# A transformer layer on eight cores: residual rows on ScalarE's DMA queue, another order ahead of the heads, and two more tiles turned by DMA

## The reference

```python
lat = rmsnorm(x @ wkv_a_w.T, norm_w)
kv = lat @ wkv_b_w.T
q = (x @ wq_w.T + wq_b).reshape(B, S, H, DH)
...
attn = softmax(where(tril, (q @ k.T) / sqrt(DH), -inf))
x = x + (attn @ v) @ out_w.T + out_b
...
gate = silu(qmm(x, gate_w, gate_scale)); up = qmm(x, up_w, up_scale)
x = x + qmm(gate * up, down_w, down_scale)
```

## Time and profile before

| | us |
|---|---|
| median of three runs | 1604.93 |
| lowest and highest of them | 1598.73 and 1613.68 |
| the profiled execution | 1596.11 |
| its span on the slowest core (core 1) | 1594.4 |
| spans of cores 0 to 7 | 1591.8, 1594.4, 1592.5, 1590.4, 1592.4, 1593.8, 1591.9, 1589.6 |
| busy on core 1: PE, DVE, ACT, POOL | 1555.1, 440.4, 363.7, 82.0 |
| the stages on core 1 begin at | heads 133.4, output rows 490.3, gate and up 596.6, down 1259.6 |

### The profile page before, as it was taken

How to read it: one execution, slowest core, us unless ns; L and a number is a source line. 1 busy time by engine, 2 the same in 40 slices (tenths; PEclk the granted TensorE clock), 3 DMA queues, 4 the chain that set the end, 5 groups by cost and what they waited for, 6 DMA issues and landing times.

```text
span 1594.4 us, 22671 instructions; the slowest of 8 cores (1589.6 to 1594.4 us)
## 1 busy us (share of the span) xinstructions
PE 1555.1 (98%) x8714; PEld 758.8 (48%) x8714; DVE 440.4 (28%) x998; ACT 363.7 (23%) x480; POOL 82.0 (5%) x174
## 2 busy tenths in 40 slices
PE   3999999999999999999999999999999999999999
PEld 2644555555555444444444444444444444444444
DVE  5735444444456661111011110111011111111111
ACT  3864565656662001101110011101110000000000
POOL 1210100000100000000000000000000000000000
PEclk9999999999999999999999999999999999999999
DMA  9953445222456995352754565372532383929210
GB/s 277 288 96 77 71 83 87 44 34 41 78 100 185 142 199 119 31 49 27 63 44 44 50 52 50 35 63 27 48 32 27 27 115 53 124 52 119 69 53 27
DMA packets 75752, 127.60 MB, mean 80 GB/s; under 512 B 46144, under 2 KB 48768, under 8 KB 70912
## 3 DMA queue, kind: packets, MB, share of 16 engines
q0 software_dynamic: 17856, 58.73, 36.6%
q1 hardware_dynamic: 57792, 67.42, 15.0%
HBM read 233.08 MB, written 16.78 MB: 157 GB/s over the span
## 4 chain that ended last, share of the span: by engine, by line
PE 91%; DMA 5%; DVE 2%; issue 1%; SPq 1%; ACT 0%; POOL 0%; DVEq 0%; ACTq 0%; POOLq 0%
PE PS L1342 21%; PE PS L1317 21%; PE PS L1323 21%; PE PS L1113 7%; PE PS L1192 4%; PE PS L1168 4%; PE PS L1122 3%; PE PS L1132 3%; PE PS L1077 3%; PE PS L1299 2%; DMA X2T<-XHb 2%; DMA WST<-wkva 1%; DMA res_scr<-RES 1%; PE PS L1141 1%; DMA X<-xq 1%
## 5 line engine op out<-in xcount | busy, mean ns | idle before, releaser
L1317 PE MATMUL PS<-X2T,W 128*128 128x512 bf16 x1536 | 347.2, 379 | 0.0
L1323 PE MATMUL PS<-X2T,W 128*128 128x512 bf16 x1536 | 347.2, 379 | 0.0
L1317 PEld LDWEIGHTS PS<-X2T,W 128*128 128x128 fp8e4 x1536 | 150.3, 98 | 181.2
L1323 PEld LDWEIGHTS PS<-X2T,W 128*128 128x128 fp8e4 x1536 | 150.3, 98 | 181.3
L880 DVE SCALAR_TENSOR_TENSOR FUSE<-PS,CF,SIL 128x512 bf16<-128x512 f32 x96 | 72.1, 751 | 587.4 <-PE PS L1323 587.4
L1032 ACT ACTIVATE SIL<-PS,CF 128x512 bf16<-128x512 f32 x96 | 66.0, 687 | 589.6 <-PE PS L1317 589.6
L957 ACT ACTIVATE P<-PS,NEGB 128x1024 bf16<-128x1024 f32 x192 | 169.9, 900 | 115.1 <-PE PS L1168 104.9
L1342 PE MATMUL PS<-WDb,FUSE 128*128 128x512 fp8e4 (+2 forms) x816 | 166.2, 366 | 0.0
L1342 PE MATMUL PS<-WDa,FUSE 128*128 128x512 fp8e4 x768 | 166.1, 379 | 0.0
L1342 PEld LDWEIGHTS PS<-WDb,FUSE 128*128 128x128 bf16 x816 | 77.9, 98 | 88.3
L1342 PEld LDWEIGHTS PS<-WDa,FUSE 128*128 128x128 bf16 x768 | 75.2, 98 | 90.6
(11 more groups left out here) (123 smaller groups left out, 946.5 us busy)
## 6 DMA issues: line engine op xcount, KB each, us to landing
W<-gu POOLq DMA_DIRECT2D x48, 512.0 KB, 9.0
WQ<-wq POOLq DMA_DIRECT2D x16, 512.0 KB, 6.7
X<-xo SPq DMA_DIRECT2D x8, 1024.0 KB, 9.1
WO<-wo POOLq DMA_DIRECT2D x16, 512.0 KB, 8.8
RES<-xq SPq DMA_DIRECT2D x8, 1024.0 KB, 7.5
res_scr<-RES SPq DMA_DIRECT2D x8, 1024.0 KB, 6.5
RB<-res_scr SPq DMA_DIRECT2D x32, 256.0 KB, 5.3
out<-OB SPq DMA_DIRECT2D x31, 256.0 KB, 2.4
```

Of the source, the lines that this page charges most:

```text
L1317: mm = e.matmul(bank(ffn_bank(f)), W8[io % 4][:, c * 128:(c + 1) * 128], X2T[:, c * 1024 + qb * 512:c * 1024 + qb * 512 + 512], start=(c = ...
L1323: mm = e.matmul(bank(ffn_bank(f) + 1), W8[io % 4][:, 2048 + c * 128:2048 + (c + 1) * 128], X2T[:, c * 1024 + qb * 512:c * 1024 + qb * 512 ...
```

## The change

It has these parts:

- **Tiles 9 and 10** are no longer transposed on PE and evicted by ACT. They are turned by DMA, as two half turns each, between the loads of tiles 12, 13 and 14 in SP's queue (`TURNED`, `turn_late`). PE waits for the landing of a turned tile where it waited for ACT (`turned`), and so does whoever writes over its XH buffer (`slot_free`).
- **Who normalises**: ACT has tiles 7 to 10; DVE has the others, 12 to 15 among them. Before, ACT had 8 to 10 and 12 to 15.
- **SP's loads**: X3 goes ahead of the first two WST, WST3 ahead of X7.
- **POOL**: WQ's load moves behind `rstd(4)`, WK's behind `rstd(8)`, and WV's behind `rstd(9)`.
- **PE's list** ahead of the heads is in another order: `rope_sum` is first; 20 and 6 matmuls of 512 columns whose results nothing reads (`warm`) are put ahead of tile 2 and behind tile 5; `lat(0, 0)`, `lat(2, 1)`, `lat(3, 0)` and `lat(3, 1)` are split, and `lat(1, ...)` no longer is; parts of `lat(3, ...)` come earlier. DVE's and ACT's lists follow it.
- **Output rows**: the spills and the RES loads of tiles 4 to 7 are issued by ACT between its roots. The load of tile t + 3 is issued after spill t, when spill t - 1 has landed.

The diff, cut in its lines of context, and without the declarations of semaphores:

```diff
@@ -82,7 +82,8 @@
-NORM_ON_ACT = (8, 9, 10, 12, 13, 14, 15)
+NORM_ON_ACT = (7, 8, 9, 10)
+TURNED = (9, 10, 12, 13, 14, 15)
...
@@ -136,7 +137,7 @@
 KIND_COUNT = {
-    "T": lambda n, half: 2 * n + half + 1,
+    "T": lambda n, half: 2 * sum(1 for k in range(n) if k not in TURNED) + half + 1,
     "Q": lambda h, qb: 2 * h + qb + 1,
...
@@ -405,6 +407,16 @@
+    def turned(n):
+
+        if n in TURNED:
+            return [(d_late[n - 8], 16)] + ([(d_late2[n - 8], 16)] if n < 12 else [])
+        return [(s_t, count(("T", n, 1)))]
+
+    def slot_free(n):
+
+        return turned(n) if n in TURNED else [(t_t, count(("T", n, 1)))]
+
     def x_count(n):
...
@@ -444,10 +456,22 @@
             src = xq_d if n < 8 else xo_d
             e.dma_start(out=X[n % 4][:, :], in_=src.ap()[(n % 8) * 128:(n % 8 + 1) * 128, :]).then_inc(d_x[n % 4], 16)
 
+        def load_constants():
+            e.dma_start(out=CF[:, :], in_=cf_d.ap()[:, :]).then_inc(d_const, 16)
+            e.dma_start(out=C2s[0:64, :], in_=c2_d.ap()[:, :]).then_inc(d_const, 16)
+            e.dma_start(out=M2s[0:64, :], in_=m2_d.ap()[:, :]).then_inc(d_const, 16)
+
         def turn_late(n):
             e.wait_ge(*normalised(n))
-            e.dma_start_transpose(out=A(XOTL, (n - 12) * 128, [[8192, 128], [512, 16], [1, 128]]),
-                                  in_=XH[n - 12][:, :]).then_inc(d_late[n - 12], 16)
+            e.wait_ge(s_cast, 4)
+            if n < 12:
+                for half in range(2):
+                    e.dma_start_transpose(out=A(XOT[half], (n - 8) * 128, [[4096, 128], [512, 8], [1, 128]]),
+                                          in_=XH[n % 4][:, half * 1024:(half + 1) * 1024]
+                                          ).then_inc((d_late if half == 0 else d_late2)[n - 8], 16)
+            else:
+                e.dma_start_transpose(out=A(XOTL, (n - 12) * 128, [[8192, 128], [512, 16], [1, 128]]),
+                                      in_=XH[n % 4][:, :]).then_inc(d_late[n - 8], 16)
 
         def load_wkva(dl):
             e.dma_start(out=WST[dl][:, :], in_=wkva_d.ap()[dl, :, :]).then_inc(d_wkva[dl], 16)
...
@@ -457,25 +481,25 @@
                         in_=xq_d.ap()[0:128, half * 1024:(half + 1) * 1024]).then_inc(d_first[half], 16)
         e.dma_start(out=CB[:, :], in_=cb_d.ap()[:, :]).then_inc(d_idb, 16)
         load_x(1)
-        e.dma_start(out=CF[:, :], in_=cf_d.ap()[:, :]).then_inc(d_const, 16)
-        e.dma_start(out=C2s[0:64, :], in_=c2_d.ap()[:, :]).then_inc(d_const, 16)
-        e.dma_start(out=M2s[0:64, :], in_=m2_d.ap()[:, :]).then_inc(d_const, 16)
+        load_constants()
         load_x(2)
+        load_x(3)
         load_wkva(0)
-        load_x(3)
         load_wkva(1)
         load_x(4)
         load_x(5)
         load_wkva(2)
         load_x(6)
+        load_wkva(3)
         load_x(7)
-        load_wkva(3)
         load_x(8)
         load_x(9)
         load_x(10)
         load_x(11)
         load_x(12)
+        turn_late(9)
         load_x(13)
+        turn_late(10)
         load_x(14)
         load_x(15)
         turn_late(12)
...
@@ -508,14 +532,9 @@
         for t in range(8):
-            e.wait_ge(v_add, 4 * (t + 1))
-            e.dma_start(out=res_d.ap()[t * 128:(t + 1) * 128, :], in_=RES[t % 4][:, :]).then_inc(d_spill[t % 4], 16)
             e.wait_ge(v_xh, 16 - len(NORM_ON_ACT) + t + 1)
                                   in_=XH2[t % 2][:, :]).then_inc(d_turn[t % 2], 16)
-            if t < 4:
-                e.wait_ge(d_spill[t % 4], 16)
-                load_res(t + 4)
         for i in range(4):
...
@@ -577,16 +596,16 @@
         rstd(2)
-        first_weights(0)
-        first_weights(1)
         rstd(3)
         rstd(4)
+        first_weights(0)
         rstd(5)
         rstd(7)
+        rstd(8)
+        first_weights(1)
+        rstd(9)
         first_weights(2)
-        rstd(8)
-        rstd(9)
         rstd(10)
...
@@ -660,7 +679,8 @@
             if n >= 4:
-                e.wait_ge(t_t, count(("T", n - 4, 1)))
+                for wait in slot_free(n - 4):
+                    e.wait_ge(*wait)
             e.tensor_scalar(XH[n % 4][:, :], X[n % 4][:, :], MV[:, 2 * n:2 * n + 1], RSTD[:, n:n + 1],
...
@@ -772,40 +792,42 @@
         stats(0)
         stats(1)
         normalise(0)
+        rope_squares()
         normalise(1)
         stats(2)
+        stats(3)
         normalise(2)
-        stats(3)
         normalise(3)
-        rope_squares()
         stats(4)
+        stats(5)
         normalise(4)
-        stats(5)
         normalise(5)
         stats(6)
         normalise(6)
+        stats(7)
         rope_weights()
-        stats(7)
-        normalise(7)
+        diagonal(0)
         stats(8)
         stats(9)
         stats(10)
-        diagonal(0)
+        evict(PLANNED[0])
         stats(11)
         latent(0)
+        stats(12)
         normalise(11)
-        evict(PLANNED[0])
-        stats(12)
         stats(13)
+        normalise(12)
         diagonal(1)
         stats(14)
+        normalise(13)
         stats(15)
+        normalise(14)
+        normalise(15)
         latent(1)
         diagonal(2)
         latent(2)
         diagonal(3)
         evict(PLANNED[11])
-        value_ones()
         latent(3)
         evict(PLANNED[13])
         evict(PLANNED[14])
...
@@ -817,8 +839,9 @@
         evict(PLANNED[21])
+        evict(PLANNED[24])
         evict(PLANNED[23])
-        evict(PLANNED[24])
+        value_ones()
         def add(t, d):
...
@@ -911,8 +934,9 @@
             e.wait_ge(g_shift, normalised(n)[1])
-            if 4 <= n and n - 4 < 12:
-                e.wait_ge(t_t, count(("T", n - 4, 1)))
+            if n >= 4:
+                for wait in slot_free(n - 4):
+                    e.wait_ge(*wait)
             e.activation(XH[n % 4][:, :], X[n % 4][:, :], AFT.Identity, bias=SHIFT[:, n:n + 1],
...
@@ -960,58 +984,53 @@
         e.wait_ge(v_eps, 1)
         e.activation(SDL[:, 0:1], EPSC[:, 0:1], AFT.Sqrt)
         transposed(0)
+        transposed(1)
         cast(0)
-        transposed(1)
-        cast(1)
         transposed(2)
         transposed(3)
+        cast(1)
         cast(2)
         transposed(4)
         e.wait_ge(d_const, 48)
         lat_out(0, 0)
+        lat_out(0, 1)
+        cast(3)
+        lat_out(0, 2)
         transposed(5)
-        cast(3)
-        transposed(6)
-        lat_out(0, 1)
-        transposed(7)
-        lat_out(0, 2)
         lat_out(0, 3)
         rms(0)
+        normalise(7)
+        transposed(6)
+        transposed(7)
         normalise(8)
         normalise(9)
         lat_out(1, 0)
+        transposed(8)
+        lat_out(1, 1)
+        lat_out(1, 2)
         normalise(10)
-        lat_out(1, 1)
-        transposed(8)
-        lat_out(1, 2)
-        transposed(9)
+        evict(PLANNED[1])
         lat_out(1, 3)
         evict(PLANNED[2])
-        evict(PLANNED[1])
-        transposed(10)
+        evict(PLANNED[3])
         rms(1)
-        evict(PLANNED[3])
         transposed(11)
-        normalise(12)
-        normalise(13)
         evict(PLANNED[4])
         lat_out(2, 0)
-        normalise(14)
+        lat_out(2, 1)
         evict(PLANNED[5])
-        normalise(15)
-        lat_out(2, 1)
-        evict(PLANNED[6])
-        evict(PLANNED[7])
-        evict(PLANNED[8])
         lat_out(2, 2)
         lat_out(2, 3)
+        evict(PLANNED[7])
+        evict(PLANNED[6])
+        lat_out(3, 0)
+        lat_out(3, 1)
+        evict(PLANNED[8])
+        lat_out(3, 2)
+        rms(2)
         evict(PLANNED[9])
+        lat_out(3, 3)
         evict(PLANNED[10])
-        lat_out(3, 0)
-        rms(2)
-        lat_out(3, 1)
-        lat_out(3, 2)
-        lat_out(3, 3)
         rms(3)
         evict(PLANNED[12])
         evict(PLANNED[17])
...
@@ -1025,6 +1044,12 @@
                     evict(job)
         for t in range(8):
             sqrt_var(16 + t)
+            e.wait_ge(v_add, 4 * (t + 1))
+            e.dma_start(out=res_d.ap()[t * 128:(t + 1) * 128, :], in_=RES[t % 4][:, :]).then_inc(d_spill[t % 4], 16)
+            if 1 <= t < 5:
+                e.wait_ge(d_spill[t - 1], 16)
+                e.dma_start(out=RES[t - 1][:, :],
+                            in_=xq_d.ap()[(t + 3) * 128:(t + 4) * 128, :]).then_inc(d_r[t - 1], 16)
         for f, (io, qb) in enumerate(FFN):
             e.wait_ge(t_g, f + 1)
             if f >= 3:
...
@@ -1036,6 +1061,10 @@
                 e.wait_ge(*evicted(before))
+
+        def warm(n):
+            for _ in range(n):
+                e.matmul(bank(3), IDB, CB[:, 0:512], start=True, stop=True)
...
@@ -1067,13 +1096,11 @@
                     e.wait_ge(s_lat, dl + 1)
                 else:
                     e.wait_ge(s_lat, 4 * tb + dl - 1)
-            if tb < 3:
-                e.wait_ge(s_t, 8 * tb + hi // 64)
-            else:
-                for i in range(hi // 128):
-                    e.wait_ge(d_late[i], 16)
+            for n in range(4 * tb, 4 * tb + hi // 128):
```

(69 more changed lines are left out.)

## The result

| | before | after |
|---|---|---|
| median (us) | 1602.55 | 1654.53 |
| ratio, with its 95% interval | | 1.031 [1.026, 1.036] |
| the profiled execution | 1596.11 | 1658.78 |
| span of the slowest core (core 1 in both) | 1594.4 | 1657.0 |
| lowest span of a core | 1589.6 | 1588.4 |

The medians here and in the table of the experiments count every execution, while the ratios leave out those in which one die ran longer at a lower granted clock (without its one such execution, the median of after is 1650.3).

A forecast was written before the change was run, and what follows sets the result against it. PE's list bounds the kernel, with almost unbroken matmuls after `scores(0)`. Gains of 2.9 us ahead of it and 2.5 in core 1's output rows leave core 5 slowest, 3.5 off the span: 1604.9 - 3.5 = 1601.4 us, whole range 1592 to 1611.

The forecast's parts named there:

- Output rows: Moving spills and later RES loads to ACT's queue removes PE's wait: 2.5 us on core 1, 0 elsewhere.
- a turn alone on SP's queue isn't held by the spill: Output rows: the reason given for taking the 2.5 us gain on core 1.
- The next square root is all that stands behind it: Output rows, ACT: the wait for a spill, one tile (13.8 us) after its issue, holds up only that root.
- Rival 2: Output rows: the spill's move is worth nothing and the 2.5 us stays; 1602.0 us, chance 0.15.
- Head of the stage: Work ahead of the heads: `scores(0)` comes 2.9 us earlier, from 0.5 + 1.8 + 1.2 - 0.6.
- The walk: PE's list on core 1 ahead of the heads, timed step by step: a lead of 0.5 us beside the 1.8.
- no wait at 80: Latent stage: PE was forecast to wait 0.6 us for turn 10, landing at 80; bounds 0 and 8 more.
- the tail's 2.2: Waits from `lat(3,3)` on, before the heads: 1.2 of 2.2 us taken as saved, bounds 0 and 2.2.
- hardly at all: PE ahead of the heads: after waiting 21.3 us in two pieces for normalised tiles, it scarcely waits again.
- Turns 13 to 15: Last turns ahead of the heads, landing at 93.2, 96.4 and 98.6: costed at nothing, the last with 1.8 us cover.
- Rival 1: Turn 15 lands late beside POOL's weight loads, PE waits 6 to 9 us; 1608 to 1611 us, chance 0.25.
- Range and chances: Whole kernel: 1592 to 1611 us; forecast 0.35; against before, faster 0.05, same 0.91, slower 0.04.

The follow-up runs named there:

- rows_on_act: The kernel before with only the output part of the change: spills and later RES loads issued by ACT; 1649.8 us, ratio 1.030.
- order_gu_late: order_loads_late with POOL's four gate and up weight loads moved from beside tiles 1 to 4 to beside tiles 4 to 7; 1597.7 us, ratio 0.996.
- rows_on_pool2: The kernel before with spills and later RES loads issued by POOL, in one queue with the W8 loads; 1644.1 us, ratio 1.024.
- order_loads_late: The change with output rows as before, and POOL's loads of the next heads' weights waiting for turns 12 to 15; 1601.8 us, ratio 0.997.
- best: order_gu_late with POOL's third and fourth gate and up loads waiting until the last turn has landed; 1599.5 us, ratio 0.997.

## Why the prediction was wrong

- **Output rows: -2.5 us on core 1, bounds 0 and 2.5.** The step that failed. It went from "a turn alone on SP's queue isn't held by the spill" to a lower bound of nothing, and no loss was weighed. The runs show +47.5 on core 1, and the whole 3% with this part alone (rows_on_act). The premise was the misreading of the earlier trace rows: I took turn 3 as slow for being *issued behind* a load and a spill. Core 1 of before, SP in order of time, about that turn:

```profile
542.34 0.38 SPq L488 DMA_DIRECT2D RES<-xq  x1
542.80 0.41 SPq L512 DMA_DIRECT2D res_scr<-RES  x1
543.31 28.91 SPq L514 DMA_TRANSPOSE X2T<-XHb  x1
```

  The load landed 23.3 us after its issue, the spill 27.3, and the W8 load of 540.2 took 18.6: all three were *in flight beside* the turn. In the kernel before this came about where SP had fallen behind, so that load and spill went out right ahead of the turn. In step and without a W8 load, the spill has at most 1.7 us left when the turn is issued, and the load is issued behind it (order_gu_late, turns of 4.2 to 4.6 us). The change issues all three ahead of each of turns 1 to 4, on every core.
- **"The next square root is all that stands behind it".** True, and beside the point: what matters of a moved transfer is what it now runs beside.
- **Rival 2** (the move is worth nothing) rested on the Trainium skill (DMA: Bandwidth & Descriptors, Issuing engines are not separate DMA queues). The runs agree with half of it: the 16 engines are shared and it doesn't matter who issues (rows_on_act 1.030 and rows_on_pool2 1.024 alike). But a second issuer didn't save only issue time, it also gave up the order that the one queue had kept, and the wait for RES grew by 47.5 us on core 1.
- **Head of the stage: -2.9 us.** The walk was right on four of the six cores where turn 15 was on time: `scores(0)` at 130.25, 129.95, 129.28 and 130.05 on cores 0, 2, 5 and 7, with 130 to 131 forecast. That is 1.2 to 4.3 us earlier than on the same cores of before. By pieces, on core 7: cast3 at 44.68 (46 forecast), its wait 1.92 (1.7), `lat(0,3)` to 50.8 (51.4), `lat(1,0)` at 58.76 (59.1) after 0.35 (0.6), no wait at 80 (0.6), and 1.2 of the tail's 2.2 left (1.0), so 1.0 saved where I took 1.2. On cores 4 and 6, whose turns were on time too, it came at 133.82 and 134.09, 1.7 and 0.6 us *later* than before. The walk had `lat(0,3)` at full rate behind the wait for cast3. There it took 5.3 us instead of 3.61, at a granted clock near 0.50 (1.2 GHz); core 6 of after, PE in order of time, and the stretch from 49 to 52:

```profile
49.35 5.29 PE L1104 MATMUL PS<-XQT,WKVA 128*128 128x512 bf16 x16 [2.16 <-ACT WKVA L955]
```

```profile
49.00:52.00 3.00, 2.65 (x7) 1.03 (x8) 2.03 (x4) 2.68 (x4) 0.00 (x0) 0.56 0.95 347
```

  Core 3 had it as well, and so had three cores of order_loads_late, two of order_gu_late and one of best. Averaged over the eight cores, `scores(0)` is at 132.5 to 133.7 in the ten profiles with the old head and at 131.7 to 133.0 in the five with the new one and its loads held back. Between the two averages lie 1.4 us, half of the 2.9. The reading that PE waits "hardly at all" after its first 21.3 us also left out 4.0 us for evictions ahead of 52 us (3.38 of them in the earlier trace rows).
- **Turns 13 to 15: nothing, with 1.8 of cover.** Rival 1 came true on cores 1 and 3: turn 15 landed after 16.7 and 18.1 us, PE waited 11.3 and 12.7 where 6 to 9 was given for it, and `scores(0)` came at 146 and 148. order_loads_late shows that POOL's loads were the cause. The argument against it, that the turn is issued 1 us ahead of them, decided it core by core: turn 15 went out 1.1 to 2.3 us ahead of the first of these loads on six cores and landed in 4.5 to 6.7; on core 3 it was 0.3 ahead, and on core 1, issued at 96.7 (about 94 forecast) against 95.6, it was behind. A lead of 1 us in a forecast over 90 us of work is no lead, and 0.25 was too low for this rival.
- **Range and chances.** 1592 to 1611 came from rivals that all took the output part as -2.5 or 0. Rival 1's price and its row (a turn 10.8 us slower beside two loads) were at hand for the output rows too: three free transfers beside each of turns 1 to 4, whose landing the normalise two tiles on waits for.

## To carry to other kernels

A queue is also an order. Before a transfer is moved to another engine's queue, list for each DMA transpose what will be in flight beside it in the new order, not only what is issued ahead of it; here a transpose of 0.5 MB bore 2 MB beside it, and with 3 or 4 it landed late on some cores. If the transfer has to move, make its issue wait for the transpose's landing, and read the landing times of all cores, since half of them can look healthy.
